# A vision tower on one core: the attention output projection in f16 products, and a feed-forward first pass with another order of loads, other batches and other scatters

## What is computed

```python
h = tok(x)                                            # (64, 196, 192)
h = h + attn0(_layernorm(h))
y = _layernorm(h)                                     # input of the feed-forward block
y1 = y + attn1(_ln(y, ln1_g, ln1_b))                  # 12 heads of 16
y2 = y1 + gelu(y1 @ mlp_w1 + mlp_b1) @ mlp_w2 + mlp_b2
xm = _ln(y2, ln2_g, ln2_b)
topv, topi = top_k(xm @ gate_w.T + gate_b, 2)         # 4 experts, two a token
y3 = y2 + sum_e comb[e] * (gelu(xm @ exp_w1[e] + exp_b1[e]) @ exp_w2[e] + exp_b2[e])
return h + y3
```

## Time and profile before

| | |
|---|---|
| time of three runs | 3161.35, 3163.67, 3172.22 us (median 3163.67) |
| the profiled execution | 3159.79 us, its span 3158.0 us |
| TensorE matmul busy | 2817.0 us, 89% of the span |
| DVE, ACT, POOL busy | 2314.7 (73%), 1872.1 (59%), 1443.2 (46%) |
| mean granted TensorE clock | 0.959 |
| DMA | 393.85 MB, mean 125 GB/s |

### The profile page before, as it was taken

How to read it: one execution, slowest core, us unless ns; L and a number is a source line. 1 busy time by engine, 2 the same in 40 slices (tenths; PEclk the granted TensorE clock), 3 DMA queues, 4 the chain that set the end, 5 groups by cost and what they waited for, 6 DMA issues and landing times. The chain is left out here.

```text
span 3158.0 us, 94811 instructions
## 1 busy us (share of the span) xinstructions
PE 2817.0 (89%) x31229; PEld 2144.8 (68%) x31229; DVE 2314.7 (73%) x5357; ACT 1872.1 (59%) x3666; POOL 1443.2 (46%) x2001
## 2 busy tenths in 40 slices
PE   4999379999999999999999985999984999999998
PEld 3888335555555555555555554999983888888887
DVE  4888467777777777777777754777774777777776
ACT  3888245666666666666666654777752444444443
POOL 2777322333333344444444411577774444444444
...
GB/s 140 159 187 128 58 103 140 133 146 148 148 150 148 155 154 162 159 161 163 157 162 161 161 104 119 147 145 142 146 121 98 66 67 67 67 67 66 67 65 49
DMA packets 514472, 393.85 MB, mean 125 GB/s; under 512 B 222432, under 2 KB 487682, under 8 KB 514178
## 3 DMA queue, kind: packets, MB, share of 16 engines
...
## 5 line engine op out<-in xcount | busy, mean ns | idle before, releaser
L657 DVE TENSOR_REDUCE a_mx<-a_mxp 98x4 f32<-98x784 f32 x768 | 746.2, 972 | 317.4 <-PE a_mxp L806 315.7
L533 ACT ACTIVATE a_pt<-a_st 98x784 f32<-98x784 f32 x768 | 631.6, 822 | 203.9 <-PE a_st L792 202.9
L1558 POOL DMA_INDIRECT out_dram<-f_yo,f_idg x202 | 332.0, 1644 | 415.9 <-DVE f_yo L1892 379.3
L479 POOL TENSOR_TENSOR a_cn<-a_ctxs,a_rec 128x392 f32<-128x392 f32 x192 | 189.7, 1016 | 533.9 <-DMA a_rec<-a_recip 533.9
L1632 ACT ACTIVATE f_hf<-f_bank,f_b1c 128x256 f32<-128x256 f32 x606 | 253.8, 472 | 236.5 <-PE f_bank L878 236.4
L868 PE MATMUL a_pr<-a_pf,a_cn 128*98 128x192 f32 x1536 | 334.4, 348 | 7.3 <-POOL a_cn L479 4.1
L821 PE MATMUL a_pv<-a_pt,a_vp 98*32 98x196 f32 x6144 | 338.1, 338 | 0.7 <-ACT a_ctxs L564 0.5
L806 PE MATMUL a_mxp<-a_kst,a_qst 48*128 48x196 f16 x3072 | 262.0, 248 | 69.2 <-DMA a_kst<-a_qk 50.2
L2048 PE MATMUL f_bank<-f_w2h,f_hh 128*128 x1212 | 298.9, 247 | 13.2 <-DVE f_hl L1876 11.6
L2049 PE MATMUL f_bank<-f_w2h,f_hl 128*128 x1212 | 298.2, 246 | 0.0
L2050 PE MATMUL f_bank<-f_w2l,f_hh 128*128 x1212 | 298.0, 246 | 0.0
(11 more groups left out here) (304 smaller groups left out, 7688.5 us busy)
## 6 DMA issues: line engine op xcount, KB each, us to landing
a_rec<-a_recip SPq DMA_DIRECT2D x256, 147.0 KB, 3.6
...
a_qst<-a_qk SPq DMA_DIRECT2D x256, 110.2 KB, 3.3
a_kst<-a_qk SPq DMA_DIRECT2D x256, 110.2 KB, 3.1
f_xg<-f_listed SPq DMA_DIRECT2D x101, 264.0 KB, 2.8
a_qk<-a_qkh SPq DMA_DIRECT2D x128, 196.0 KB, 2.8
a_qk<-a_qkl SPq DMA_DIRECT2D x128, 98.0 KB, 2.9
a_qk<-a_qkh SPq DMA_DIRECT2D x128, 98.0 KB, 2.4
```

The costliest lines, as they stand in the source:

```text
L533: act.activation(pt[k % PT][:].rearrange("p j a t -> p j (a t)"), st_ps[0:half_t, :, 0:unit_t], ACT.Exp, scale=sm_scale).then_inc(exp_s, 1)
L657: dve.tensor_reduce(mx[:, a, :, 2 * p:2 * p + 2].rearrange("p q j -> p j q"), mx_ps[0:half_t, :, 0:unit_t].rearrange("p j (q t) -> p j q t ...
L1558: pool.indirect_dma_start(out, bass.IndirectOffsetOnAxis(ap=idg[i % 3][:, t:t + 1], axis=0), yo[i % 3][:, t, :], None, compute_op=ALU.add) ...
```

## The change

Attention's projection: `cn` becomes f16 and holds, for each head's 32 rows, the high part of 16 values in the first half and the low part in the second. For this `vp` is laid out so that a head's 32 columns stand 12 apart, its values are repeated in it by a DMA a unit (`twice`), and row 31 of each head is at first the sum and then, by another DMA (`dup`), the repeated 16th value. POOL makes `cn` with three operations of 1176 columns. `project` uses, for each x, six f16 matmuls (three groups, high and low weights) and one for the bias; two x share a PSUM tile and one DVE operation. The slot constants change. Ahead of the steps there are an extra turned block of weights and its split in high and low parts, two more bias loads a layer and a few constants.

Feed-forward, pass one: SP loads the first unit ahead of the weights, then the b1 arrays, the second unit and the other small arrays; each engine's preparations that need the small arrays move behind step 0; two memsets (5280 and 2112 columns) move from DVE to POOL; the `acc` addition moves from POOL to DVE; the list of batches has 16 entries for 12; `idx` has four buffers and `place_rows` waits for the batch three back; and at even steps from 35 on a further unit is scattered if its batch is placed a step or more.

The diff, cut to the parts above (the preparations moved into functions behind step 0, the constants and the semaphores are left out), indented eight less:

```diff
@@ -143,7 +149,9 @@
-cn = [sb(f"cn{i}", [128, 3, unit_t], F32) for i in range(2)]
+cf = sb("cf", [128, 3, unit_t], F32)
+ch = sb("ch", [128, 3, unit_t], F16)
+cn = [sb(f"cn{i}", [128, 3, unit_t], F16) for i in range(2)]
@@ -197,16 +207,16 @@
-OUTS, NORM, REC = 4, 5, 64
-ROWS_AT, TURN_AT, VALUES_AT = (9, 11, 6), (3, 5), (1, 2)
-PROJECT_AT = ((2, 2, 2), (4, 4, 4), (6, 6, 6), (9, 10, 10))
-HIGH_PART_AT, VALUES_OUT_AT = (4, 6), (1, 2)
-LOW_PART_AT, LOW_ROWS_AT, OUT_AT = (4, 7), (9, 11, 6), (3, 4, 7, 11)
+OUTS, NORM, REC = 2, 5, 64
+ROWS_AT, TURN_AT, VALUES_AT = (9, 11, 6), (2, 3), (0, 1)
+PROJECT_AT = (4, 4, 6, 6)
+HIGH_PART_AT, VALUES_OUT_AT = (3, 6), (1, 2)
+LOW_PART_AT, LOW_ROWS_AT, OUT_AT = (4, 7), (10, 11, 6), (4, 8)
...
-ROWS_FIRST, PART_FIRST, CONTEXT_FIRST, VALUES_FIRST = (1, 1, 0), (0, 1), (1, 1, 1, 1, 1, 1), (0, 0)
-NEGATED_AT, RECIP_AT, STATS_AT, AGGREGATE_AT = 6, 4, (10, 0), 2
+ROWS_FIRST, PART_FIRST, CONTEXT_FIRST, VALUES_FIRST = (0, 1, 0), (1, 1), (0, 1, 1, 0, 0, 1), (0, 0)
+NEGATED_AT, RECIP_AT, STATS_AT, AGGREGATE_AT = 6, 5, (9, 1), 4
@@ -355,19 +366,27 @@
+                  (cn_s, 3 * u - 2),
...
+            b = (par + 1) % 2
+            sp.dma_start(ctxs[b][2 * hd - 1::32], ctxs[b][hd - 1::32]).then_inc(dup_s, 16)
...
-                  (cn_s, 3 * u),
+                  (cn_s, 3 * u - 2),
...
+            u, b = s + 1, (par + 1) % 2
+            waits(sp,
+                  (pv_s, GROUPS * (u - 1) + 1),
+                  (vp_s, 2 * (u + 1)))
+            sp.dma_start(vp[b][:, :, dim:2 * dim - heads], vp[b][:, :, 0:dim - heads]).then_inc(twice_s, 16)
@@ -474,10 +498,16 @@
+            wait(pool, cn_s, 3 * u)
+            wait(pool, dup_s, 16 * (u + 1))
...
-            for g in range(3):
-                pool.tensor_tensor(cn[b][:, g, :], ctxs[b][:, g, :], rec[:, g, :], ALU.mult).then_inc(cn_s, 1)
+            pool.tensor_tensor(cf[:], ctxs[b][:], rec[:], ALU.mult).then_inc(cn_s, 1)
+            pool.wait_ge(cn_s, 3 * u + 1)
+            pool.tensor_tensor(ch[:], cf[:], low_half[:].unsqueeze(2).to_broadcast([128, 3, unit_t]), ALU.mult).then_inc(cn_s, 1)
+            pool.wait_ge(cn_s, 3 * u + 2)
+            pool.tensor_tensor(cn[b][:], cf[:], ch[:], ALU.subtract).then_inc(cn_s, 1)
+    pool.wait_ge(set_s, 12)
@@ -541,8 +571,8 @@
-        order = "p (x h d) -> p x h d" if layers[layer][7] else "p (x d h) -> p x h d"
-        act.copy(vp[b][:, 2 * n:2 * n + 2, :, 0:hd],
+        order = "p (x h d) -> p x d h" if layers[layer][7] else "p (x d h) -> p x d h"
+        act.copy(vp[b][:, 2 * n:2 * n + 2, 0:dim].rearrange("p x (d h) -> p x d h", h=heads),
@@ -598,16 +631,25 @@
-        dve.tensor_reduce(praw[layer][:, :, :, hd + 1:hd + 2], pbv[:], AX.X, ALU.add).then_inc(p_ok[layer], 1)
+        dve.tensor_copy(praw[layer][:, :, :, hd:2 * hd], praw[layer][:, :, :, 0:hd]).then_inc(p_ok[layer], 1)
+        for part in range(2):
+            dve.tensor_reduce(pbias[layer][:, :, 32 * part:32 * part + 1], pbv[:].rearrange("p e h d -> p e (h d)"),
+                              AX.X, ALU.add).then_inc(p_ok[layer], 1)
...
+        dve.wait_ge(w_f[layer], G_READY[layer] + 4)
+        dve.tensor_copy(ph[layer][:], pf[layer][:]).then_inc(w_ok[layer], 1)
+        dve.wait_ge(w_ok[layer], 3)
+        dve.tensor_tensor(pl[layer][:], pf[layer][:], ph[layer][:], ALU.subtract).then_inc(w_ok[layer], 1)
+        dve.wait_ge(w_ok[layer], 4)
+        dve.tensor_copy(pl[layer][0:32, 3, :], ph[layer][0:32, 3, :]).then_inc(w_ok[layer], 1)
...
-            dve.wait_ge(p_ok[0], 3)
+            dve.wait_ge(p_ok[0], 5)
@@ -693,14 +735,15 @@
-        dve.scalar_tensor_tensor(out=xo[b][:, x, :], in0=pr_ps[0:half_t, 0:dim], scalar=1.0 / WSCALE,
-                                 in1=xres[b][:, x, :], op0=ALU.mult, op1=ALU.add).then_inc(xo_s, 1)
+        dve.scalar_tensor_tensor(out=xo[b][:, 2 * x:2 * x + 2, :], in0=pr_ps[0:half_t, 0:2 * dim].rearrange("p (t d) -> p t d", t=2),
+                                 scalar=1.0 / (WSCALE * WSCALE), in1=xres[b][:, 2 * x:2 * x + 2, :],
+                                 op0=ALU.mult, op1=ALU.add).then_inc(xo_s, 1)
...
-    pe.wait_ge(consts, 10)
+    pe.wait_ge(consts, 13)
@@ -818,7 +860,7 @@
-                ins = pe.matmul(pv_ps[32 * h4:32 * h4 + 32, 0:tok], vp[b][:, 2 * a + kt, h, :], pt[(first + h4) // 2 % PT][:, h4 % 2, kt, :],
+                ins = pe.matmul(pv_ps[32 * h4:32 * h4 + 32, 0:tok], vp[b][:, 2 * a + kt, :].rearrange("p (c h) -> p c h", h=heads)[:, :, h], pt[(first + h4) // 2 % PT][:, h4 % 2, kt, :],
@@ -860,14 +902,16 @@
-    def project(u, b, x, g, layer):
-        if g == 0:
-            wait(pe, xo_s, OUTS * u + x)
+    def project(u, b, x, layer):
+        if x % 2 == 0:
+            wait(pe, xo_s, OUTS * u + x // 2)
...
-            wait(pe, cn_s, 3 * u + g + 1)
-        ins = pe.matmul(pr_ps[0:half_t, 0:dim], cn[b][:, g, x * half_t:(x + 1) * half_t], pf[layer][:, g, :],
-                        start=(g == 0), stop=(g == 2))
-        if g == 2:
+            wait(pe, cn_s, 3 * (u + 1))
+        ts, at = slice(x * half_t, (x + 1) * half_t), x % 2 * dim
+        ins = products(pe, pr_ps[0:half_t, at:at + dim],
+                       [(ones16[:], pl[layer][:, 3, :])]
+                       + [(cn[b][:, g, ts], w[layer][:, g, :]) for g in range(3) for w in (ph, pl)])
+        if x % 2 == 1:
@@ -1220,7 +1264,7 @@
-    sizes = [5] * 9 + [2, 1, 1]
+    sizes = [5] * 6 + [3, 2, 2, 2, 1, 3, 2, 2, 1, 1]
@@ -1306,7 +1350,7 @@
-idx = [sb(f"idx{i}", [P, BMAX, 2], U32) for i in range(2)]
+idx = [sb(f"idx{i}", [P, BMAX, 2], U32) for i in range(4)]
@@ -1430,11 +1476,13 @@
+    load_unit(0)
...
-    load_unit(0)
-    sp.wait_ge(consts, 1)
+    for f in [MLP, *range(n_exp)]:
+        sp.dma_start(b1c[:, f, :], b1s[f].rearrange("(c p) -> p c", p=P), allow_slow_non_contiguous=True).then_inc(b1_in if f == MLP else small_in, 16)
+    load_unit(1)
+    sp.wait_ge(consts, 4)
...
-        sp.dma_start(b1c[:, f, :], b1s[f].rearrange("(c p) -> p c", p=P), allow_slow_non_contiguous=True).then_inc(small_in, 16)
@@ -1535,15 +1585,14 @@
-            wait(pool, x4_s, u + 1)
-            wait(pool, x_in[u % 4], 48 * (u // 4 + 1))
-            wait(pool, out_s, 16 * (u - 2))
-            pool.tensor_tensor(acc[u % 3][:], x4[u % 3][:], hres[u % 4][:], ALU.add).then_inc(acc_s, 1)
...
+            done += 1
+        if s >= 35 and s % 2 == 0 and done < NU and first_unit[batch_of[done]] + sizes[batch_of[done]] - 1 <= s - 6:
+            scatter(done, range(2))
@@ -1595,8 +1645,9 @@
+    high_tokens(0)
...
-    high_tokens(0)
+    act.wait_ge(b1_in, 16)
@@ -1611,6 +1662,8 @@
+        if s == 0:
+            small_parts()
@@ -1691,6 +1742,8 @@
+        wait(dve, out_s, 16 * (u - 2))
+        dve.tensor_tensor(acc[u % 3][:], x4[u % 3][:], hres[u % 4][:], ALU.add).then_inc(acc_s, 1)
@@ -1749,7 +1802,7 @@
-            wait(dve, sc_s[j], 16 * (first_unit[b - 1] if b else 0))
+            wait(dve, sc_s[j], 16 * (first_unit[b - 3] if b >= 3 else 0))
```

More of the change, by code:

```diff
@@ L109, in attention_phase @@
         wl = [sb(f"wl{i}", [128, 2, 3 * dim], F16) for i in range(NL)]
-        pf = [sb(f"pf{i}", [128, 3, dim], F32) for i in range(NL)]
+        pbias = [sb(f"pbias{i}", [rows_q, 2, 128], F32) for i in range(NL)]
+        pf = [sb(f"pf{i}", [128, 4, dim], F32) for i in range(NL)]
+        ph = [sb(f"ph{i}", [128, 4, dim], F16) for i in range(NL)]
+        pl = [sb(f"pl{i}", [128, 4, dim], F16) for i in range(NL)]
         bq = [sb(f"bq{i}", [128, QB], F32) for i in range(NL)]
@@ L136, in attention_phase @@
         kst = [sb(f"kst{i}", [128, pairs, 2, tok + PAD], F16) for i in range(2)]
-        vp = [sb(f"vp{i}", [half_t, 4, heads, 32], F32) for i in range(2)]
+        vp = [sb(f"vp{i}", [half_t, 4, 32 * heads], F32) for i in range(2)]
         mx = sb("mx", [half_t, 2, 2, heads], F32)
@@ L261, in attention_phase @@
             G_READY.append(W_READY[-1] if affine is None else W_READY[-1] + 2)
[L262 removed]
+            W_LOADS.append((18 if head_major else 3) + 2 + 4 + 1 + (2 * 3 if affine is not None else 0))
         def halves(rows):
@@ L420, in _ @@
             for layer in range(NL):
-                pool.memset(praw[layer][:], 0.0).then_inc(consts, 1)
+                pool.memset(pbias[layer][:], 0.0).then_inc(consts, 1)
             pool.memset(ident[:], 0.0).then_inc(consts, 1)
@@ L500, in prepare @@
                         act.mul(wg[:, part, :], wf[layer][:, part, :], gcol[:, part:part + 1]).then_inc(w_f[layer], 1)
-                for n in range(3):
+                for n in range(4):
                     act.wait_ge(w_t[layer], n + 5)
@@ L774, in step @@
                         for x in range(4):
-                            for g in range(3):
-                                if PROJECT_AT[x][g] == k:
-                                    project(s - 2, par, x, g, kinds["Y"])
+                            if PROJECT_AT[x] == k:
+                                project(s - 2, par, x, kinds["Y"])
```

(13 more changed lines are left out.)

114 lines of the change are left out of this document (67 added, 47 removed).

## The result

The changed kernel is slower: 3266.6 us in the median of 4 runs (3254.1 to 3277.0) against 3166.3 for the kernel before (3161.4 to 3172.2), a ratio of 1.030 with a 95% interval of 1.025 to 1.036. The profiled execution took 3254.1 us, its span is 3252.2, 94.2 longer than before. The forecast was 3178, in a range of 3126 to 3204.

A forecast was written before the change was run, and what follows sets the result against it. A loop through SP was taken to bound each attention step, with SP itself and the context loop close. Attention +36 and feed-forward −19.5 on 3159.8 made 3176, given as 3178 us, range 3126 to 3204.

The forecast's parts named there:

- the steps' assumption of a full clock: Attention steps were priced from windows at the full granted clock; the sum held no term for a falling clock.
- Step 2: Attention, SP queue: the two new issues cost 1.4 us a step (bounds 1.0 and 1.65), +18 us in layer 1.
- Projection: Attention, TensorE: f16 matmuls of 2.3 us a step replace f32 ones of 4.3, freeing 2.0 us a step.
- step 3: Attention, POOL: three context operations take 9.0 us instead of 2.98, +8 us over the 22 layer 0 steps.
- The context loop: Attention, from SP's store through POOL's products and projection to QK's rows: 23.0 us, +0.36 a step in layer 0.
- DVE and ACT: Attention's residual sums and value copies: equal work, under DVE's 53 of 68 us busy, so nothing.
- Start, end, unrolled steps: Attention outside the loops: unrolled steps +0.2 each, +2 us; start +5 (bounds 2 and 8); end +3.
- the rival with the weight load: Attention's weighted sums: strided weight loads cost +22 us, giving 3192 to 3215, say 3200; chance 12%.
- Feed-forward start: Before pass one: tokens and MLP weights load first, so the first product comes earlier, −10.5 us.
- Batches: Feed-forward scatters: fewer units left at the end −15 us, POOL's lag +5, sixteen batches instead of twelve +1.
- The rival that SP has hidden room: Attention, SP queue: gaps hide waits for TensorE, whose freed 2.0 us set the step; 3110 to 3150; chance 35%.
- The rule on 16-byte lines: Weighted sums' strided weight loads: accesses outside one SBUF line pay extra, putting the sum some 20 us higher.

The follow-up runs named there:

- Run 2: Kernel before with only the projection in f16 (24 matmuls a unit, the context's low part left out): ratio 1.004 to the kernel before.
- run 5: Changed kernel with the values repeated by a second ACT copy out of PSUM instead of SP's `twice` DMA: ratio 1.000 to the kernel before.
- run 1: Kernel before with only two new DMAs a unit on the SP queue, like `dup` and `twice`: ratio 1.041 to the kernel before.
- run 11: Kernel before with the f16 projection, each product computed twice (48 f16 matmuls a unit): ratio 1.003 to the kernel before.
- run 12: Changed kernel with ACT copying the values and issuing `dup`, neither on SP, and unit 2 loaded early: ratio 0.993 to the kernel before.
- run 7: Kernel before with the changed feed-forward part and unit 2's load moved ahead of the expert weights: ratio 0.993 to the kernel before.
- run 3: Kernel before with only the strided layout of the values (a head's columns 48 bytes apart): ratio 1.002 to the kernel before.
- run 6: Changed kernel with 14 dummy f16 matmuls twice a step where TensorE waits for the maxima rows: ratio 1.035 to the kernel before.
- run 17: Kernel of run 12 with 4 dummy f16 matmuls twice a step where TensorE waits for the maxima rows: ratio 0.999 to the kernel before.
- run 18: Kernel of run 12 with 8 dummy f16 matmuls twice a step where TensorE waits for the maxima rows: ratio 1.002 to the kernel before.
- run 4: Kernel before with only the changed feed-forward part, on a chip where the kernel before takes 3186 us: ratio 1.006 to the kernel before.

## Why the prediction was wrong

The direction was given the largest chance, 0.46; the size was missed by 89 us and the range by 63. Attention was forecast at +36 and took +105.9. Of the 70 us between them the steps' assumption of a full clock has the most: 25 us in the looped steps, and most of the 41 by which the unrolled ones exceed their +2 (points 5 and 6). Step 2's issues have 8, and start and end give 4 back. The other 19 are the feed-forward part (8.5) and the choice of profile: the profiled execution was the fastest of four, 12.5 below their median, where 2 was allowed. By the steps of the prediction:

1. **Projection.** Right in what it removes, and wrong in what that is worth. TensorE's busy time in a step at full clock fell by 1.3 us in layer 0 and 1.2 in layer 1 (from 21.4), of the 2.0 forecast. Run 2, without new issues, shortens the steps at full clock by only 0.3 us, where 22.1 and 21.8 were expected from 22.7 and 22.6, and shows that even this is no gain in sum.
2. **SP issues. This step failed by its size**: 1.4 us with a bound of 1.65, while the rows show 0.64 + 1.20 = 1.84. `twice` was sized by an issue of the same 98 partitions (0.35, or 0.62 for its four pieces a row), with 0.25 for its waits: it takes 0.93, and 0.27 to the next. The L379 issue, 0.35, also fetches four pieces of 768 bytes for each partition, from DRAM; why a copy within SBUF takes 0.93 is not shown. With 1.84 the step's own formula gives 22.05 + 1.84 = 23.9 in layer 1 and 21.1 + 1.84 = 22.9 in layer 0; the clean steps are (23.41 + 24.49) / 2 = 23.95, and 22.9. That they agree so well is in part luck: SP's waits show that its own work before was 21.6 in layer 1 and not 22.05, that it grew by 2.1, and that it still waits 0.25. In the looped steps at full clock the measured steps make +28 in layer 1, where +18 stood, and +6 in layer 0, where +8 stood for another cause (step 3).
3. **POOL.** Forecast 9.0, measured 7.4. The context loop does not bind: with the same three operations layer 0 steps come down to 21.9 in run 5. What stood as +8 for layer 0 came from SP in fact (0.26 x 22 = 6).
4. **DVE and ACT.** Nothing, as said: DVE's busy time in the two stretches is 392 and 424 us for 388 and 428, ACT's 321 and 350 for 332 and 362.
5. **Start, end, unrolled steps.** The start of attention to its first `rec` took 0.7 (forecast 5), the end behind the last `rec` 3.3 (forecast 3). The failure is "unrolled +0.2 each": the 17 intervals outside the two loops took 43.0 us more in sum (6.4, 22.5 and 14.1), with clocks of 0.63 to 0.93 in 12 of them (3 before). Most of it goes with `twice`: without it, in run 5, they take 12 more than before.
6. **The missing term.** The steps were summed at a full clock; **this is the step that failed by the most**. The parts: 22 layer 0 steps +16.7, of which 5.7 at full clock and 11.0 by falls (two falls of before taken off); 24 of layer 1 +42.2, of which 28 at full clock and 14 by falls, each step taken at 23.95; +43.0 elsewhere; 0.7 and 3.3: 105.9. A fall was named in one half sentence of the rival with the weight load, with a price of 0.35 a step. TensorE at 95% busy was read as the sign of a bound; by runs 1, 2 and 11 it was also what kept the clock up. A step that adds waiting and takes work away at once (20 us busy in 24) lost both. The busy share alone doesn't tell how often it falls: in layer 1 TensorE is busy 90% of a step at full clock both in run 12, with one fall in 24 steps, and in run 1, with twelve.
7. **Feed-forward start.** The first product came 11.1 us earlier (10.5 forecast), but only 2.4 of it reached the first residual: it was asked what covers the preparations, and not what is late next. Unit 2's load stands behind 13 small ones, four of expert weights and three of zero rows; run 7 shows the price, 22.0 - 14.8 = 7.2 us.
8. **Batches.** Tail −16.2 (−15 forecast), pass one +7.6 (+6 forecast): right on this chip. Feed-forward together −11.0, not −19.5, nearly all by step 7 (8.1 of 8.5).

The rival that SP has hidden room fell: its gap of 0.88 us before L423 stood in the changed kernel too (1431.08 to 1431.96), with 0.2 us of waiting in it. It comes in every second step only, where the written order of the two-step loop ends, so it looks like the loop's own time. SP did have more room than was read, 1.1 us for 0.67, and for TensorE too (the L404 row), but 1.84 us filled it. The rule on 16-byte lines (the Trainium skill, SBUF — State Buffer, Door 1: The DMA port swizzle) bears out in the load's length, 109 to 151 ns in run 3, and not in the time: +0.2% at an interval that takes in zero.

What settles the main cause: two SP issues alone bring the loss (run 1), taking them away step by step brings clean steps from 23.8 to 22.8 and 22.3 in layer 1 and the ratio from 1.030 to 1.000 and 0.993 (runs 5 and 12; 6 to 7 us of the last are unit 2's), and falls come with TensorE's idle time and lessen with dummy work (runs 2, 11, 6, 17, 18). What is left open: why some chips run pass one at 427 and 464 us instead of 405 and 413, with waits that no record explains; there the new feed-forward part is a loss. What in TensorE's idle time decides whether the clock falls, its share or the length of single waits, was not separated, and neither was why the unrolled steps at the layer change lose most.

The fastest that was run, beside the kernel before on the same chip, are run 7 (0.993, attention as before, the new feed-forward part with unit 2 early) and run 12 (0.993); run 7 is the simpler one, and where pass one is disturbed neither can be expected to hold that: run 4 gave 1.006, and runs 17 and 18, close to run 12, gave 0.999 and 1.002.
